# First conditioned batch by channel halves, and the rows of two tiles ahead of the weights in the second expert layer

## The reference

```python
decay = exp(-exp(w)) * (0.5 + 0.5 * tf)          # tf = sigmoid(sum(cond)), one per batch
ek, ekv = exp(minimum(k, 30)), exp(minimum(k, 30)) * v   # k = v = fside
nf, df = scan(a * decay + ekv), scan(b * decay + ek)     # forward over the 256 tokens
nb, db = the same scans in reverse
euk = exp(minimum(u + k, 30))
num, den = nf + nb - ekv + euk * v, df + db - ek + euk
out = sigmoid(x) * (num / maximum(den, 1e-8)) * (0.8 + 0.2 * tf)
x = x + attention_0(out)    # then experts_0, attention_1, experts_1, each on its own conditioned x
```

```python
h = gelu(x @ W1 + b1); h = gelu(h @ W2 + b2); eo = h @ W3 + b3
out = sum over the 2 chosen experts of eo * gate
```

## Time and profile before

| | us |
|---|---|
| median of 3 runs | 1159.49 |
| lowest, highest | 1157.91, 1161.74 |
| the profiled execution | 1154.83 |
| its span | 1153.0 |
| PE busy in the span | 977.0 (85%) |
| DVE busy | 807.0 (70%) |
| ACT busy | 581.1 (50%) |
| POOL busy | 211.7 (18%) |

### The profile page before, as it was taken

The page is one execution under the profiler, slowest core; times in us unless marked ns, Lnnn a source line. Parts: engine busy times, 40 slices in busy tenths (PEclk is TensorE's granted clock), DMA queues, the critical chain, the costliest instruction groups (busy, mean ns, idle before and its releaser), DMA issues.

```text
span 1153.0 us, 18483 instructions
## 1 busy us (share of the span) xinstructions
PE 977.0 (85%) x6328; PEld 699.4 (61%) x6328; DVE 807.0 (70%) x2080; ACT 581.1 (50%) x1444; POOL 211.7 (18%) x175
## 2 busy tenths in 40 slices
PE   1889888988898889889988989779898985998995
PEld 1667666766676667664555656523332464987884
DVE  6678878887788778884388887567667772454542
ACT  2388638863786378631233332146566733454442
POOL 1101020102010201027333333100000050322223
PEclk9999999999999999979999999979999987999998
DMA  9999700000000000024488885515464548676772
GB/s 264 247 231 232 162 1 1 1 1 2 1 2 1 1 1 2 1 103 167 141 267 271 284 270 165 187 73 217 149 219 167 199 152 292 209 241 195 235 217 28
DMA packets 75965, 161.30 MB, mean 140 GB/s; under 512 B 10706, under 2 KB 57310, under 8 KB 71776
## 3 DMA queue, kind: packets, MB, share of 16 engines
q1 hardware_dynamic: 66992, 145.52, 41.0%
q0 software_dynamic: 8880, 14.60, 4.9%
HBM read 127.68 MB, written 62.62 MB: 165 GB/s over the span
## 4 chain that ended last, share of the span: by engine, by line
PE 50%; DVE 16%; DMA 14%; ACT 9%; issue 6%; POOL 3%; SPq 1%; ACTq 0%; POOLq 0%; DVEq 0%
PE ps L1658 46%; DMA out<-arena 7%; DMA arena<-in_w0all 3%; DMA made<-arena 3%; DVE arena L1439 2%; POOL out L532 2%; ACT arena L633 1%; ACT arena L618 1%; DVE arena L1107 1%; POOL slots L521 1%; DVE arena L1069 1%; ACT arena L626 1%; PE ps L1758 1%; ACT arena L611 1%; DVE arena L1131 1%
## 5 line engine op out<-in xcount | busy, mean ns | idle before, releaser
L1658 PE MATMUL ps<-arena 128*128 128x256 f16 (+15 forms) x4712 | 769.4, 339 | 62.7 <-ACT arena L626 19.6
L1658 PEld LDWEIGHTS ps<-arena 128*128 128x128 f32 (+8 forms) x4712 | 527.6, 148 | 234.9 <-issue 98.4
L1642 DVE CAST arena<-arena 128x256 f16<-128x256 f32 x120 | 37.2, 310 | 95.9 <-ACT arena L845 95.9
L1439 DVE TENSOR_REDUCE arena<-ps 128x4 f16<-128x1024 f32 (+1 forms) x48 | 58.8, 1228 | 49.8 <-PE ps L1658 49.7
L845 ACT ACTIVATE arena<-ps,arena 128x256 f32<-128x256 f32 x120 | 55.6, 474 | 57.9 <-PE ps L1658 56.0
L1131 DVE SCALAR_TENSOR_TENSOR arena<-arena 128x128 f32<-128x128 f32 x240 | 84.0, 412 | 0.7 <-issue 0.3
L469 POOL TENSOR_TENSOR den<-den,backd 128x512 f32<-128x512 f32 x8 | 10.5, 1308 | 402.9 <-DVE euv L947 402.9
L633 ACT ACTIVATE arena<-ident,arena 128x128 f32<-128x128 f32 x256 | 81.0, 391 | 0.0
L532 POOL DMA_INDIRECT out<-arena x30 | 47.3, 1577 | 146.6 <-DMA out<-arena 76.7
L1098 DVE SCALAR_TENSOR_TENSOR arena<-arena,ps 128x128 f32<-128x128 f32 (+1 forms) x128 | 47.2, 410 | 37.7 <-PE ps L1658 31.5
L501 POOL DMA_INDIRECT made<-arena x47 | 53.0, 1128 | 103.1 <-DVE arena L1352 102.1
(11 more groups left out here) (281 smaller groups left out, 1258.4 us busy)
## 6 DMA issues: line engine op xcount, KB each, us to landing
arena<-split SPq DMA_DIRECT2D x14, 2048.0 KB, 9.2
arena<-in_w0all SPq DMA_DIRECT2D x47, 608.0 KB, 5.1
slots<-in_blank SPq DMA_DIRECT2D x17, 1040.0 KB, 16.0
arena<-in_w1all SPq DMA_DIRECT2D x16, 1024.0 KB, 6.6
split<-arena SPq DMA_DIRECT2D x32, 512.0 KB, 3.8
slots<-in_blank SPq DMA_DIRECT2D x9, 1072.0 KB, 18.8
arena<-slots SPq DMA_DIRECT2D x47, 130.0 KB, 3.6
side<-made SPq DMA_DIRECT2D x8, 512.0 KB, 5.4
```

The source lines that it names most:

```text
L1439: dve.tensor_reduce(out, ps[:, at:at + 2].rearrange("p j (r s) -> p j r s", r=nr), X, ALU.max, negate=True).then_inc(max1_done, 1)
L1658: return pe.matmul(o, l, r, start=start, stop=stop, skip_group_check=shared)
```

## The change

Four things change. (1) At the entry the bounding of the other batches' columns leaves its place between the scans of slice 0 and stands behind the conditioned batch 0. (2) The reciprocals, the product into `fac` and the conditioning of batch 0 go by channel half: two reciprocals, product, conditioning of half 0, and then the same for half 1. PE's `hidden0(0)` goes over k outer and c inner, waits for half 0 (`c_dve` 7) and then for half 1 (`xc_ready` 1), and puts two blocks into one bank with one start of accumulation. (3) On ACT the exponential of the other batches' columns stands behind the tanh of batch 0. (4) In the second expert part SP issues the rows of tile 1 directly behind those of tile 0, ahead of the second and third layers' weights of tile 0.

```diff
--- before.py
+++ after.py
@@ -443,8 +443,8 @@
             tile_weights(0)
             sp.wait_ge(scattered, 16 * 2 * TAU)
             tile_rows(0)
+            tile_rows(1)
             tile_weights(0, 1)
-            tile_rows(1)
             tile_weights(1)
             sp.wait_ge(base_ready, 4)
             sp.dma_start(out[0:NT].rearrange("(a p) c -> p a c", p=P), base).then_inc(base_out, 16)
@@ -553,9 +553,6 @@
                 act.activation(euk[:], euk[:], ACT.Exp).then_inc(euk_out, 1)
 
             exp_slice(0)
-            act.wait_ge(c_dve, 7)
-            act.activation(ek[:, :, T:], ek[:, :, T:], ACT.Exp).then_inc(c_act, 1)
-
             def sigmoid_batch(b):
                 if b:
                     act.wait_ge(xc_ready, b)
@@ -568,6 +565,8 @@
                 act.activation(oT.rearrange("p a t -> p (a t)"), ps[:, 3], ACT.Copy).then_inc(tail_act, 1)
 
             sigmoid_batch(0)
+            act.wait_ge(c_dve, 8)
+            act.activation(ek[:, :, T:], ek[:, :, T:], ACT.Exp).then_inc(c_act, 1)
             for b in range(B):
                 for h in range(2):
                     act.wait_ge(projected, b * PROJ0 + 1 + h)
@@ -968,20 +967,30 @@
 
                 def finish():
                     dve.wait_ge(*done["invert"])
-                    if first:
-                        dve.wait_ge(sums_out, nth + 1)
                     st(dve.scalar_tensor_tensor(
                         fac[:, bass.ds(i, 1), :, cols].rearrange("p i c t -> p (i c) t"), num[:],
                         oscale[:, bass.ds(b, 1)], den[:], ALU.mult, ALU.mult))
                     st.settle()
 
-                def rest_bounded():
-                    dve.wait_ge(ld["x"], 48)
-                    cs(dve.tensor_scalar(ek[:, :, T:], kT[:, :, T:], 30.0, None, ALU.min))
+                def finish_first(c):
+                    if c == 0:
+                        dve.wait_ge(sums_out, nth + 1)
+                    dve.wait_ge(*done["invert"])
+                    st(dve.scalar_tensor_tensor(fac[:, 0, c, cols], num[:, c], oscale[:, 0:1], den[:, c],
+                                                ALU.mult, ALU.mult))
+                    st.settle()
+                    if c == 0:
+                        dve.wait_ge(sig_ready, 1)
+                    ins = dve.scalar_tensor_tensor(xc[:, c], sig[:, c], 1.0, fac[:, 0, c, cols], ALU.add, ALU.mult)
+                    if c == 0:
+                        cs(ins)
+                    else:
+                        st.tell(ins, xc_ready, 1)
 
                 if first:
-                    return [lambda: forward(num, ekv), rest_bounded, lambda: backward(backn, ekv), own_term, lambda: forward(den, ek),
-                            lambda: backward(backd, ek), first_sums, floor, *(lambda q=q: invert(q) for q in range(4)), finish]
+                    return [lambda: forward(num, ekv), lambda: backward(backn, ekv), own_term, lambda: forward(den, ek),
+                            lambda: backward(backd, ek), first_sums, floor, lambda: invert(0), lambda: invert(1),
+                            lambda: finish_first(0), lambda: invert(2), lambda: invert(3), lambda: finish_first(1)]
                 return [*([] if early else [shifted]), lambda: forward(num, ekv), lambda: forward(den, ek),
                         lambda: backward(backn, ekv), lambda: backward(backd, ek),
                         *([early_own_term, early_sums] if early else [own_term]), floor, *(lambda q=q: invert(q) for q in range(4)), finish]
@@ -996,7 +1005,8 @@
                         xc_ready, count)
 
 
-            condition_batch(0, 0, 1)
+            dve.wait_ge(ld["x"], 48)
+            cs(dve.tensor_scalar(ek[:, :, T:], kT[:, :, T:], 30.0, None, ALU.min))
             dve.wait_ge(c_act, 4)
             st(dve.tensor_tensor(ekv[:, :, T:], ek[:, :, T:], kT[:, :, T:], ALU.mult))
             split = []
@@ -1662,9 +1672,20 @@
 
             def hidden0(b):
 
+                if b == 0:
+                    for k in range(CT):
+                        if k == 0:
+                            pe.wait_ge(c_dve, 7)
+                        else:
+                            pe.wait_ge(xc_ready, 1)
+                        for c in range(4):
+                            ins = mm(ps[:, 6 + c // 2, (c % 2) * T:(c % 2 + 1) * T], dw1[:, k, c * P:(c + 1) * P],
+                                     xc[:, k], k + c % 2 == 0, k == CT - 1, True)
+                            if k and c % 2:
+                                ins.then_inc(projected, 1)
+                    return
                 pe.wait_ge(xc_ready, b + 1)
-                if b:
-                    pe.wait_ge(tail_act, (b - 1) * 6 + 2)
+                pe.wait_ge(tail_act, (b - 1) * 6 + 2)
                 for c in range(4):
                     for k in range(CT):
                         ins = mm(ps[:, 6 + c // 2, (c % 2) * T:(c % 2 + 1) * T], dw1[:, k, c * P:(c + 1) * P],
```

## The result

The changed kernel takes 1152.12 us (median of 5 runs, 1151.66 to 1157.90); the kernel before, in the same comparison, 1161.74 (1157.91 to 1164.05). The ratio is 0.9943, with a 95% interval of 0.9919 to 0.9967: 6.6 us less, between 3.8 and 9.4. Forecast were 8.2 us less and 1151.3 us. Two more comparisons gave 0.9924 [0.9895, 0.9952] and 0.9935 [0.9911, 0.9958], or 8.8 and 7.5 us less. The size agrees with the forecast within the interval. The way there does not in all points.

A forecast was written before the change was run, and what follows sets the result against it. TensorE was taken to stand still at the entry and for tile 1's rows in the second expert layer. 1154.83 - 5.07 - 3.1 = 1146.7, plus 4.66 for the median, gives 1151.3 us; range 1147.3 to 1156.2.

The forecast's parts named there:

- The clock at the start: Entry, PE's first 16 records: kept at 5.56 us; 1.9 us gained if all fast, 1.7 lost if all at half speed.
- The table load: Entry, ACT: 1.28 us by its row, gelus done at 26.75; by the skill's 2.66, PE loses an estimated 0.1 us.
- what is late next: Second expert layer: tile 2's rows still land at 972.5, PE waits there, and 3.1 of the 5.3 us remain.
- the stores follow this turn at an unchanged distance: Second expert layer: stores follow PE up to tile 2, so the chain in `out` moves by 3.1 us as well.
- clock case: Rival, chance 0.18: lower clock in tile 0's second layer leaves 2.3 us, entry loses 1.3; 6.1 remain, 1153.4 us.
- The chain of stores: Second expert layer: ACT, hence PE's pace, starts stores up to tile 2; from there it goes landing to landing in `out`.

The follow-up runs named there:

- e1: The kernel before, run again with no edit; ratio to before 0.9981 [0.9954, 1.0009].
- e8: The kernel before, third profile with no edit; ratio to before 1.0008 [0.9987, 1.0028].
- e3: The kernel before with only the new order of rows in the second expert layer; ratio 1.0004 [0.9984, 1.0024].
- e12: The changed kernel plus 20 unread products on PE between tile 0's second layer and the turn of tile 2; ratio to before 0.9927 [0.9897, 0.9956].
- e9: The changed kernel, third profile with no edit; ratio to before 0.9935 [0.9911, 0.9958].
- e11: The changed kernel with seven unread DVE additions delaying the first product, run a second time; ratio to before 0.9982 [0.9963, 1.0002].
- e5: The kernel before with only the bounding moved and its exponential behind the tanh; ratio 0.9931 [0.9892, 0.9971].
- e2: The changed kernel without the new order of rows in the second expert layer, entry only; ratio to before 0.9956 [0.9933, 0.9979].
- e6: The changed kernel with the rows of tile 2 also ahead of the weights of tile 1; ratio to before 0.9881 [0.9816, 0.9945].
- e10: The changed kernel with tile 2's rows also ahead of tile 1's weights, run a second time; ratio to before 0.9899 [0.9865, 0.9933].

## Why the prediction was right, and where it was not

**The total.** 6.6 us were measured and 8.2 forecast, and the interval of 3.8 to 9.4 holds both. That the sum fits so well is in part luck: by the stretches of fourteen profiles the entry gave more than its forecast, and two later stretches took some of it away, one of them unforeseen.

**Entry: the mechanism right, one wait longer than its row.** From the scans to the first product it is 4.94 us less in the profile after, forecast 5.07. The bounding gives 2.87 (forecast 2.77), the halves 2.07 (2.30): the product into `fac` takes 0.49 over half the columns where 0.42 was taken from another line, and starts 0.11 behind the reciprocals. The clock at the start made no difference that counts: 5.70 against 5.56 for the 16 records, and over the profiles 5.40 to 6.71 with an early start and 5.22 to 6.24 with a late one. The table load cost what its row says, 1.28, with the gelu 1.29 behind its start; the 2.66 us of the Trainium skill (ScalarE: Activation LUTs, What ACT_TABLE_LOAD costs) do not show here. The prediction was right in that, but the earlier trace rows could not tell: there ACT idles for 13.73 us behind the load.

What one profile of before could not tell is how long DVE waits for the identity ahead of the bounding. It is 1.89 us in that profile, and 3.60, 2.12 and 4.08 us in e1, e8 and e3:

```profile
12.16 0.96 DVE L980 TENSOR_SCALAR side<-side 128x1536 f32<-128x1536 f32 x1 [4.08 <-DMA ident<-in_ident]
```

So from scans to first product the old entry takes 17.41, 19.12, 17.64 and 19.58 us, and the new one, which no longer waits for that load, 12.46 or 12.47 in all seven profiles that have it unheld. The gain is 6.0 us on average, and 4.9 only in the best case for the old entry. The times agree without being able to weigh it: 5.1 us (2.4 to 7.8) for the entry alone, and 5.4 lost when it is held back.

**The first expert layer: not foreseen, and not settled.** The prediction named no stage between as one that could answer to an earlier start. In the seven profiles with a late first product the stretch takes 138.88 to 141.25 us, mean 140.39; in the seven with an early one 139.08 to 144.54, mean 142.15, or 1.8 us more. PE's waits for the weights of this layer add up to 16.4 us on average in the first seven (14.2 to 17.7) and to 18.1 in the others (16.5 to 20.0), which would account for it. At the end of the layer most of the gain is still there: the last store comes at 711.20 to 714.02 us in all the early profiles and at 714.38 to 719.45 in all the late ones, 3.3 us apart on average. But the samples are single executions, the stretches overlap, no run changed those waits alone, and the times are too coarse to show 1.8 us. So it stays open whether a third of the gain is given back here.

**Second expert layer: the rows right, the clock behind them missing.** The gain up to the turn of tile 1 is 4.9 us (14.34 to 9.42 after the last scatter; forecast 5.3), the second layer follows, and what is late next are the rows of tile 2, as named. In the profile after they land 24.20 us after the last scatter where 23.45 was forecast, which leaves 2.39 us of gain. Over the samples PE turns tile 2 at 27.66 us after the last scatter in the five profiles with the old order and at 24.82 in the six with the new one (e12 left out): 2.8 us, close to the forecast of 3.1.

What failed is the step behind it, that the stores follow this turn at an unchanged distance. From the turn to the first store it is 5.91 or 5.92 us in all five profiles with the old order, and 7.28 to 8.85 in five of the six with the new one, because the granted clock falls to 1.2 GHz behind or, in e3 and e9, already in the pause for the rows, for some 3.4 us or, once, for nearly 7. In e11 it did not fall, with a pause of 3.10, and there the distance is 5.93. On average this takes 1.6 us, and 1.3 us of the 2.8 are left at the first store: 33.6 us against 32.3.

The prediction had a clock case, but put it only at the second layer of tile 0, and took the pause of 2.09 us for evidence that a pause of 2 us is harmless. It is not always: in e5 the clock falls behind a pause of 2.02 us at that very place. Its price was also misread. The 24 products of 4.08 us do not all run at the lower clock, since it is back at 2.4 GHz from 967 on the earlier trace rows and they end at 968.30; in e1 and e2, where it stays low for nearly all of them, they take 5.16 and 5.20 us. By these, 48 products all at the lower clock would take an estimated 10.4 us, not 8.2, and the case would keep 0.1 us of gain instead of 2.3. In e5 the lower clock lasted for a part of them only, and they took 7.08. The warning of the Trainium skill (TensorE: Matmul & The Clock Gate, HAM oscillation), that pauses for DMAs bring PE back to its lower clock, was set aside too early.

That the low clock costs 1.7 us is shown: the same products to the first store take 7.59 us with it in the profile after and 5.93 without it in e11 and e12. That the pause brings it down is supported, not proved. The clock stayed up in all three profiles in which the pause was gone or shortened to 1.19 us (e6, e10, e12), and fell in five of the six in which it was there. But e11 is the sixth, and of the waits of 1.35 to 2.09 us ahead of the second layer one in fourteen came with the fall. So the length of the pause alone does not decide.

The chain of stores, taken to follow PE up to tile 2, did so in the one profile before alone: in e1, e8, e2 and e5, all in the old order, the store of tile 2 already waits for the landing of tile 1's, as it does after the change. This costs the forecast nothing that shows. From the first store to the end it is 172.5 us on average in the old order and 172.0 in the new one, and the landings keep their length (8.80 to 10.62 us in the profile before, 8.48 to 10.53 in the profile after).

In the time, the order alone gives nothing that can be measured (1.0004, from 1.9 us less to 2.8 us more), and beside the entry 0.9956 became 0.9924 on one chip, within the intervals.

**The range.** By its own rule (1149.1 less 1.6 to 1154.4 plus 2.2) it runs from 1147.5 to 1156.6 and not from 1147.3 to 1156.2; the measured 1152.12 lies inside both.

**The version that comes out best** is that of e6 and e10: with the rows of tile 2 ahead of the weights of tile 1 the pause is gone, the clock stays, and 28.4 us remain on average from the last scatter to the first store. Its times were 0.9881 and 0.9899 of the kernel before, 0.36% (about 4 us) below the changed kernel in the comparison that had both, with intervals that overlap.

## What to carry to other kernels

A small transfer that gates a matrix engine belongs ahead of the large ones, but then ask which small transfer is behind the same large ones next: here moving one row load only moved the wait by one tile, and moving two removed it. Price a new pause of the matrix engine twice, once for its length and once for the clock behind it; in this kernel 2.4 us of waiting cost 1.7 us more, in most executions though not in all. A wait for a load read from one profile is one sample; here it was between 1.89 and 4.08 us. And where single executions differ by as much as the gain, cut the span into stretches and compare each over several profiles, before a stretch of one profile is explained.

## What the runs showed of the hardware

The granted clock did not react to a pause in a fixed way. It fell with waits of 2.38, 2.43, 2.49, 3.43 and 3.67 us for the rows of tile 2 and with one of 2.02 us ahead of the second layer (e5). It did not fall with one of 3.10 us for those rows (e11), nor with the other waits ahead of the second layer, of 1.35 to 2.09 us. It was back after some 3.4 us, once after nearly 7. No run here shows what decides between the two. The table loads at the entry of e5, e6 and the changed kernel took 1.28 us each, and the next activation started 1.29 us behind the load's start.
